# Causal mask of a 16-head attention as 26 more contraction rows of the score products, in place of mask matmuls

## The reference

```
att = jnp.einsum('bthd,bThd->bhtT', q, k) / math.sqrt(HD)
causal = jnp.triu(jnp.ones((Tx, Tx), bool), 1)
att = jnp.where(causal, -jnp.inf, att)
att = jax.nn.softmax(att, axis=-1)
out = jnp.einsum('bhtT,bThd->bthd', att, v).reshape(Bx, Tx, Cx)
return out @ Wo + bo
```

## Time and profile before

| | |
|---|---|
| median of 3 runs | 1179.05 us (1177.37 to 1180.38) |
| profiled execution: first to last instruction | 1175.3 us |
| profiled execution: its own time | not listed apart; the three runs lie 2.1 to 5.1 us above the span |
| PE / DVE / ACT / POOL busy, share of the span | 91% / 63% / 51% / 40% |
| attention of layer 0 | about the first 474 us of the span |
| mean granted PE clock | 0.953 of full |

### The profile page before, as it was taken

One profiled execution on the slowest core, in us unless ns is written; L12 is line 12 of the kernel. 1 busy time (PEld: TensorE's weight loads), 2 busy tenths in 40 slices (PEclk: granted clock), 3 DMA queues, 4 the chain that ended last, 5 costly groups with the idle time before them and its releaser, 6 DMA issues. The chain is left out here.

```text
span 1175.3 us, 19800 instructions
## 1 busy us (share of the span) xinstructions
PE 1067.3 (91%) x6630; PEld 603.4 (51%) x6630; DVE 734.6 (63%) x1549; ACT 596.7 (51%) x1133; POOL 467.8 (40%) x692
## 2 busy tenths in 40 slices
PE   5699999999999998479999974899999998999997
PEld 3244455454454443336565642566666665455654
DVE  2867878787787783624332322767787874566756
ACT  3167667676767666113332322443444442876752
POOL 2444635444453511068888874323333420000000
PEclk9599999999999999579999996999999998999999
DMA  4531414233250411436766672021210002001001
GB/s 150 99 58 18 87 37 89 65 70 82 52 105 21 73 40 47 155 103 138 162 162 135 138 154 71 6 65 42 76 39 26 35 15 95 1 10 63 28 28 54
DMA packets 73540, 85.05 MB, mean 72 GB/s; under 512 B 12560, under 2 KB 67800, under 8 KB 73312
## 3 DMA queue, kind: packets, MB, share of 16 engines
q1 hardware_dynamic: 61088, 66.99, 21.9%
q0 software_dynamic: 12288, 16.79, 8.4%
q10 hardware_dynamic: 64, 0.02, 0.0%
HBM read 45.31 MB, written 25.21 MB: 60 GB/s over the span
## 5 line engine op out<-in xcount | busy, mean ns | idle before, releaser
L566 DVE TENSOR_REDUCE nmax<-psum 128x1 f32<-128x512 f32 (+3 forms) x352 | 215.6, 637 | 44.6 <-PE psum L790 39.8
L683 ACT ACTIVATE pT<-psum 128x512 f32<-128x512 f32 x320 | 181.2, 596 | 65.5 <-PE psum L811 35.5
L788 PE MATMUL psum<-k6T,q6T 96*128 96x512 bf16 (+3 forms) x512 | 128.7, 312 | 15.2 <-DVE nmax L566 11.3
L808 PE MATMUL psum<-q6T,k6T 99*128 99x512 bf16 x320 | 119.3, 382 | 1.1 <-ACT pT L683 0.9
L1093 POOL DMA_INDIRECT residual<-expert_y,idx_e x64 | 101.3, 1583 | 25.2 <-issue 17.1
L1612 DVE TENSOR_TENSOR l_scores<-psum,const_sb 128x512 f32<-128x512 f32 x128 | 79.5, 684 | 19.1 <-PE psum L1787 19.0
L788 PEld LDWEIGHTS psum<-k6T,q6T 96*128 96x128 bf16 x512 | 46.0, 100 | 88.4 <-DVE nmax L566 55.2
L790 PE MATMUL psum<-negs_bf,ident_bf 128*128 128x128 bf16 (+2 forms) x352 | 89.0, 253 | 0.0
L823 PE MATMUL psum<-pT,v 128*32 128x512 f32 x640 | 85.0, 604 | 0.0
L1080 POOL DMA_INDIRECT expert_tokens<-router_input,idx_e x64 | 63.2, 987 | 50.0 <-POOLq L913 30.8
L1745 PE MATMUL psum<-l_hT,l_w 128*128 128x512 f32 x128 | 66.4, 643 | 1.6 <-ACT l_hT L1680 0.9
(11 more groups left out here) (298 smaller groups left out, 2245.4 us busy)
## 6 DMA issues: line engine op xcount, KB each, us to landing
q6T<-q_parts SPq DMA_DIRECT2D x96, 128.0 KB, 4.3
expert_w<-in_ew SPq DMA_DIRECT2D x16, 768.0 KB
x_in<-in_x SPq DMA_DIRECT2D x8, 512.0 KB, 4.2
residual<-x SPq DMA_DIRECT2D x32, 128.0 KB, 1.9
router_input<-h SPq DMA_DIRECT2D x32, 128.0 KB, 1.8
l_x<-residual SPq DMA_DIRECT2D x8, 512.0 KB, 6.6
x_dram<-l_x SPq DMA_DIRECT2D x32, 128.0 KB, 1.7
out<-c_out SPq DMA_DIRECT2D x16, 256.0 KB, 2.1
```

What stands on the lines that cost most here:

```text
L566: dve.tensor_reduce(nmax[:, i, u * nh:(u + 1) * nh], ps_s[:, n % SR, 0:nh * (i + 1) * P].rearrange("p (h k) -> p h k", h=nh), AX_X, ALU.ma ...
L683: act.activation(pT[:, n % PR].rearrange("p h t -> p (h t)"), ps_t[:, n % TR, :], ACT.Exp, scale=HD ** -0.5).then_inc(probs, 1)
L788: pe.matmul(out[:, a, :], q6T[0:6 * HD, b % 2, u * nh + a, i * P:(i + 1) * P], k6T[0:6 * HD, b % 2, 0:w], start=a == 0, stop=False, skip_g ...
L808: last = pe.matmul(out, k6T[:, b % 2, j * P:(j + 1) * P], q6T[:, b % 2, hg * 4:hg * 4 + 4, i * P:(i + 1) * P], start=True, stop=j < i)
```

## The change

The mask moves into the contraction. 26 more rows (96 to 121) are added to `q6T` and `k6T`; the three rows of maxima move to 122 to 124. On the query side these rows hold powers of two that depend only on a query's place in its tile; on the key side they hold powers of two of the other sign, so that the product is hugely negative where the key is after the query. The 128 places are cut into 5 segments of 26 or 25.

- S: the mask product L790 is gone. The product of each head has 122 contraction rows in place of 96.
- ST on the diagonal: L811 is gone. In its place the product is split in two, over segments 0, 2, 4 (3 x 26 queries of 4 heads) and segments 1, 3 (2 x 25 queries), each with key tiles of its own.
- `k6T` now has 15 tiles of 128 per sequence buffer: masked, plain, even-segment and odd-segment copies of the keys. ACT fills them with three copies per sequence (L747, L748, L751 of the new kernel) where there was one.
- At the start one more DMA brings the mask constants, POOL writes them with 11 casts in front of its first `st` step, and SP places the query rows in `q6T` with two DMAs in front of the list of steps.
- Two DVE casts and a DVE memset at the start go.

```diff
-        k6T = sb("k6T", [6 * HD + 3, 2, T], BF16)
+        k6T = sb("k6T", [P, 2, K_TILES * P], BF16)
+        mask = sb("mask_rows", [P, 5, P])
+        phi = sb("mask_queries", [P, T], BF16)
...
+def parted(v, first, count):
+
+    lo, size = SEGMENTS[first]
+    return bass.AP(v.tensor, v.offset + lo * v.ap[-1][0], [list(v.ap[0]), list(v.ap[1]), [51 * v.ap[-1][0], count], [v.ap[-1][0], size]])
...
+                sp.wait_ge(mask_ready, 1)
+                for s in range(2):
+                    sp.dma_start(q6T[K_ROWS:MASK_ROWS, s], phi[K_ROWS:MASK_ROWS, :].unsqueeze(1).to_broadcast(
+                        [MASK_ROWS - K_ROWS, H, T])).then_inc(mask_placed[s], 16)
...
+                pool.wait_ge(mask_loaded, 16)
+                settle(pool, m.passed)
+                pool.tensor_copy(phi[K_ROWS:P, :].rearrange("p (i t) -> p i t", i=NT),
+                                 mask[K_ROWS:P, 4:5, :].to_broadcast([P - K_ROWS, NT, P])).then_inc(mask_ready, 1)
+                for s in range(2):
+                    for n, at, count_of in ((0, own_tile(0), 3), (0, own_tile(3), 1), (1, plain_tile(0), 3), (2, even_tile(0), 4),
+                                            (3, odd_tile(0), 4)):
+                        pool.tensor_copy(k6T[K_ROWS:P, s, at * P:(at + count_of) * P].rearrange("p (i t) -> p i t", i=count_of),
+                                         mask[K_ROWS:P, n:n + 1, :].to_broadcast([P - K_ROWS, count_of, P])).then_inc(mask_ready, 1)
+                pool.wait_ge(mask_ready, 11)
+                settle(pool, m.passed)
                 pool.wait_ge(ready, 1)
...
-                        act.activation(k6T[0:6 * HD, b % 2, :], ps_x[0:6 * HD, x_use[s] % XR].bitcast(BF16)[:, 0:T],
+                        turned = ps_x[0:K_ROWS, x_use[s] % XR].bitcast(BF16)
+                        act.activation(k6T[0:K_ROWS, b % 2, 0:plain_tile(0) * P], turned[:, 0:plain_tile(0) * P], ACT.Copy)
+                        act.activation(k6T[0:K_ROWS, b % 2, plain_tile(0) * P:even_tile(0) * P], turned[:, 0:T],
                                        ACT.Copy).then_inc(x_drain, 1)
+                        act.wait_ge(x_drain, x_use[s] + 1)
+                        act.activation(k6T[0:K_ROWS, b % 2, even_tile(0) * P:K_TILES * P].rearrange("p (two t) -> p two t", two=2),
+                                       k6T[0:K_ROWS, b % 2, plain_tile(0) * P:even_tile(0) * P].unsqueeze(1).to_broadcast([K_ROWS, 2, T]),
+                                       ACT.Copy).then_inc(keys_masked, 1)
...
                         for a in range(nh):
-                            pe.matmul(out[:, a, :], q6T[0:6 * HD, b % 2, u * nh + a, i * P:(i + 1) * P],
-                                      k6T[0:6 * HD, b % 2, 0:w], start=a == 0, stop=False, skip_group_check=True)
-                        pe.matmul(out[:, :, i * P:w], m.ident_bf[:], m.negs_bf[:].unsqueeze(1).to_broadcast([P, nh, P]),
-                                  start=False, stop=True, skip_group_check=True).then_inc(s_fill, 1)
+                            last = pe.matmul(out[:, a], q6T[0:MASK_ROWS, b % 2, u * nh + a, i * P:(i + 1) * P],
+                                             keys[:, first:first + step_by * i + 1:step_by, :], start=a == 0, stop=True,
+                                             skip_group_check=True)
+                        last.then_inc(s_fill, 1)
...
-                        last = pe.matmul(out, k6T[:, b % 2, j * P:(j + 1) * P],
-                                         q6T[:, b % 2, hg * 4:hg * 4 + 4, i * P:(i + 1) * P], start=True, stop=j < i)
-                        if j == i:
-                            last = pe.matmul(out, m.ident_bf[:], m.negt_bf[:].unsqueeze(1).to_broadcast([P, 4, P]),
-                                             start=False, stop=True)
-                        last.then_inc(t_fill, 1)
+                        queries = q6T[0:ALL_ROWS, b % 2, hg * 4:hg * 4 + 4, i * P:(i + 1) * P]
+                        if j < i:
+                            pe.matmul(out, keys(plain_tile(j)), queries, start=True, stop=True).then_inc(t_fill, 1)
+                        else:
+                            pe.wait_ge(keys_masked, b + 1)
+                            pe.matmul(parted(out, 0, 3), keys(even_tile(i)), parted(queries, 0, 3), start=True, stop=True,
+                                      skip_group_check=True)
+                            pe.matmul(parted(out, 1, 2), keys(odd_tile(i)), parted(queries, 1, 2), start=False, stop=True,
+                                      skip_group_check=True).then_inc(t_fill, 1)
```

More of the change, by code:

```diff
@@ L31 @@
 EPS = 1e-5
-NEG = -1e30
 ROWS, ROW_GATE_A, ROW_SHIFT_B, ROW_SCALE_B, ROW_GATE_B, ROW_GATE_L1 = 5, 0, 1, 2, 3, 4
@@ L36 @@
 C_IDENT, C_ROPE = 0, 128
-C_NEGS = C_ROPE + NT * 2 * HD
-C_NEGT, C_KEEP, C_BD, C_SEQ, C_SGN, C_PARITY, C_HEADS = (C_NEGS + n for n in (128, 256, 384, 512, 513, 514, 516))
+C_KEEP = C_ROPE + NT * 2 * HD
+C_BD, C_SEQ, C_SGN, C_PARITY, C_HEADS = (C_KEEP + n for n in (128, 256, 257, 258, 260))
 C_SPREAD = C_HEADS + KC * 32
@@ L56, in rope_rows, with own_tile, plain_tile, even_tile @@
     return np.repeat(table, P // HD, axis=1).transpose(1, 0, 2)
+SEGMENTS = ((0, 26), (26, 25), (51, 26), (77, 25), (102, 26))
+K_ROWS = 6 * HD
+MASK_ROWS = K_ROWS + 26
+ALL_ROWS = MASK_ROWS + 3
+K_TILES = 15
+def own_tile(i):
+    return i if i < NT - 1 else 2 * NT - 2
+def plain_tile(j):
+    return NT - 1 + j
+def even_tile(i):
+    return 2 * NT - 1 + i
+def odd_tile(i):
+    return 3 * NT - 1 + i
+def mask_rows():
+    MID, STEP = 54, 27
+    n = MASK_ROWS - K_ROWS
+    c = np.zeros((5, 32, P), np.float64)
+    s = np.arange(P)
+    def masks(chosen, exponents, out):
+        for r in range(n):
+            at = [lo + r for lo, size in (SEGMENTS[j] for j in chosen) if r < size]
+            passed = sum((s > t).astype(int) for t in at)
+            for k, e in zip(range(1, len(at) + 1), exponents if len(at) == len(exponents) else exponents[::2]):
+                out[r, passed == k] = -2.0 ** (e - MID)
+    masks(range(5), [19 + STEP * j for j in range(5)], c[0])
+    masks((0, 2, 4), [26, 26 + 2 * STEP, 19 + 4 * STEP], c[2])
+    masks((1, 3), [26 + STEP, 26 + 3 * STEP], c[3])
+    for j, (lo, size) in enumerate(SEGMENTS):
+        for r in range(size):
+            c[4, r, lo + r] = 2.0 ** (MID - STEP * j)
+    c[0:4, n:n + 3] = 1
+    return c.transpose(1, 0, 2).astype(np.float32)
 def shape_constants():
@@ L195, in attention_phase @@
         c_loaded = sem("att_c_loaded")
+        mask_loaded = sem("att_mask_loaded")
+        mask_ready = sem("att_mask_ready")
+        keys_masked = sem("att_masked_keys_ready")
+        mask_placed = [sem(f"att_mask_placed{s}") for s in range(2)]
         mod_loaded = [sem(f"att_wmod_loaded{n}") for n in range(2)]
@@ L226, in attention_phase @@
         qs = sb("q_parts", [P, 2, 3, T], BF16)
-        q6T = sb("q6T", [6 * HD + 3, 2, H, T], BF16)
+        q6T = sb("q6T", [P, 2, H, T], BF16)
         nmax = sb("nmax", [P, NT, H])
@@ L351, in _ @@
                 sp.dma_start(wmod[:, :, 0:2 * C], m.d["wmod"][:, 0, :, 0:2 * C]).then_inc(mod_loaded[0], 16)
-                sp.dma_start(m.const[:, 0:C_NEGS], m.d["const"][:, 0:C_NEGS]).then_inc(const_loaded[0], 16)
+                sp.dma_start(m.const[:, 0:C_KEEP], m.d["const"][:, 0:C_KEEP]).then_inc(const_loaded[0], 16)
+                sp.dma_start(mask[K_ROWS:P], m.d["mask"]).then_inc(mask_loaded, 16)
                 for dst, name in early:
                     sp.dma_start(dst[:], m.d[name]).then_inc(w_loaded[0], 16)
-                sp.dma_start(m.const[:, C_NEGS:C_END], m.d["const"][:, C_NEGS:C_END]).then_inc(const_loaded[1], 16)
+                sp.dma_start(m.const[:, C_KEEP:C_END], m.d["const"][:, C_KEEP:C_END]).then_inc(const_loaded[1], 16)
                 sp.dma_start(wmod[:, :, 2 * C:6 * C], m.d["wmod"][:, 0, :, 2 * C:6 * C]).then_inc(mod_loaded[1], 16)
@@ L780, in step @@
                         if first_scores[b, u * nh // 8] == s:
+                            pe.wait_ge(mask_ready, 11)
+                            pe.wait_ge(mask_placed[b % 2], 16)
                             pe.wait_ge(x_drain, x_use[("kT", b)] + 1)
@@ L785, in step @@
                         w = (i + 1) * P
-                        out = ps_s[:, n % SR, 0:nh * w].rearrange("p (h k) -> p h k", h=nh)
+                        out = ps_s[:, n % SR, 0:nh * w].rearrange("p (h k t) -> p h k t", h=nh, t=P)
+                        keys = k6T[0:MASK_ROWS, b % 2, :].rearrange("p (k t) -> p k t", t=P)
+                        first, step_by = own_tile(i), 1
+                        if i == NT - 1:
+                            first = plain_tile(0)
+                        if i == 1:
+                            step_by = plain_tile(0) - own_tile(1)
                         for a in range(nh):
-                            pe.matmul(out[:, a, :], q6T[0:6 * HD, b % 2, u * nh + a, i * P:(i + 1) * P],
```

(10 more changed lines are left out.)

15 lines of the change are left out of this document (5 added, 10 removed).

## The result

The kernel after took 1157.82 us (median of 4 runs, 1157.64 to 1161.28), the kernel before 1179.38 in the same session (1177.37 to 1180.38). The ratio is 0.9832 with the interval 0.9816 to 0.9849: 19.8 us faster by the ratio and 21.6 by the medians, where 25.3 was forecast. The profiled execution is the slowest of the four (1161.28 us, span 1159.4), at a mean granted clock of 0.949 where the other three had 0.954 to 0.956.

The account below looks back on a forecast made before the run. The prediction took PE to bound the steady attention, with DVE 10.5 us behind. Gains of 35.1 us less additions of 5.4, 2.4 and 2.0 gave -25.3 from 1179.05, so 1154 us, range 1138 to 1168.

Parts of the forecast that it names:

- PE is the bound before, and removing 7.0 us of it helps: Steady attention: PE busy 51.53 of 52.60 us a period; the mask products removed are 7.0 us per sequence.
- I take 48.0, near the DVE end: Period of the steady attention: 48.0 us, between 45.6 and 48.3; gain 4.6 per period, 27.6 over six.
- At 45.6 DVE would be 92% busy without any of its waits: Reason given for a period near the DVE end, 48.0 us, instead of the 45.6 with PE still the bound.
- The part behind the last key copy, 4.1 + 0.9: Last sequence after its key copy: 4.1 us gained on remaining score steps, 0.9 on eight diagonal steps.
- I take 2.5, between 0 and 7.0: First sequence's scores, before the key copy of sequence 1: 2.5 us gained, between 0 and 7.0.
- Casts on POOL, +5.4: Start: eleven casts ahead of POOL's first step add 5.4 us uncovered, between 3.3 and 9.8.
- ACT copies, +2.4: Three key copies instead of one delay queued exponentials: 0.3 us per sequence, between 0 and 1.7; in all +2.4.
- The split pair, +2: Diagonal ST steps: uneven run starts cost 0.015 us per step over 128 steps, +2; upper end +82.
- PE stays the bound: Rival for the steady attention: DVE's S waits end with PE's masks; 1131 to 1135 us, chance 0.12.
- The ring rival: DVE and ACT steps keep their places, holding PE at 50 us a period, copies at full cost; 1165 to 1179, chance 0.14.
- The slow pair: Rival: split diagonal products run slowly, deciding from 0.21 us excess a step; 1234 us at the f32 end, chance 0.06.
- the change without effect: Rival: PE waits at every S for its bank, freed time becomes waits, only additions stay; 1189 us, chance 0.02.

Follow-up runs that it names:

- masks_gone: The kernel before without both mask products (causal mask left out) and with nothing added: 1150.8 us, ratio 0.9771.
- q_late_before: The kernel before with DVE's query products moved behind up to two reductions, nothing else: 1171.9 us, ratio 0.9937.
- combo: The changed kernel with mask casts behind POOL's first st step, query products behind up to two reductions, third key copy in ACT's gap: 1134.3 us.
- dve_short3: The changed kernel with DVE's S reduction reading only the first half of each head's keys: 1152.7 us, ratio 0.9794.
- q_late3: The changed kernel with each DVE query product moved behind up to two following S reductions or h2 steps: 1144.9 us, ratio 0.9716.
- pool_late3: The changed kernel with POOL's eleven mask casts behind its first st step instead of in front: 1152.9 us, ratio 0.9786.
- third_gap3: The changed kernel with ACT's third key copy moved into its wait between the two query casts: 1153.3 us, ratio 0.9790.
- no_third: The changed kernel without the third key copy, the diagonal pair reading the plain keys (mask left out of ST): 1151.6 us, ratio 0.9793.
- one_pair: The changed kernel with the split diagonal pair as one 512-column product on the plain keys (mask left out of ST): 1155.0 us, ratio 0.9800.
- combo4: combo with DVE's query products allowed behind up to four reductions or h2 steps instead of two: 1135.7 us, ratio 0.9645.

## Why the prediction was right, and where its sizes were off

**PE is the bound before, and removing 7.0 us of it helps.** Right in the main. PE was busy 98% of a period, and masks_gone shows 4.1 us less a period from the removal alone. But 1.1 of the 52.1 us was already DVE's order (q_late_before), so PE alone would have allowed 44.0 or less, and the prediction's 45.6 for that case was too high. That combo stands at 45.7 is partly coincidence.

**"I take 48.0, near the DVE end."** The term was mis-sized: 48.8 measured. The additions hold 0.75 of it (48.80 against 48.05 in masks_gone), so the removal by itself came to 48.05 where 48.0 was forecast. Moving the third copy gives 0.54 back, so most of the 0.75 is that copy, which I had priced at 0.3 per sequence in a term of its own. And I counted 4.6 from the late period of 52.6, six times, though the mean of the six was 52.1; the first one took only 50.6. The gain was 20.0 instead of 27.6: 4.8 of the difference is the new period, 2.8 the old one.

**"At 45.6 DVE would be 92% busy without any of its waits."** The value chosen was near, but this reason failed, so that the number is near is luck. The period is not held by DVE's load: dve_short3 took it to 67% and gained 0.5 us a period. What holds it are two stalls in DVE's fixed order, one behind the other: the wait at the query product, while a reduction stands ready behind it, and then the h instruction, which takes 1.5 us in place of 0.5 beside a POOL instruction. PE waits 0.66 us for the reduction behind the first and 0.79 behind the second. I had written that the wait would shrink little, which is what happened (20.3 to 19.5 us), but took it as a fixed cost beside the load and not as a cause of the 48; the second stall isn't in the prediction at all. With both removed, in combo, DVE runs at 38.82 of 45.80 us, 85%, and PE hardly waits. q_late3 and combo removed them together, and no run removed one alone.

**The part behind the last key copy, 4.1 + 0.9.** 5.0 measured, from that copy to the router. The two terms were not measured apart.

**"I take 2.5, between 0 and 7.0", the part in front of sequence 1's copy.** In the profiled execution it lies outside the stated bounds: 1.3 us lost. The row to read was the clock. The windows from the first score to the copy of sequence 1, of before and of masks_gone (the clock is the third number from the right):

```profile
34.00:79.80 45.80, 37.08 (x183) 17.16 (x183) 32.33 (x59) 16.91 (x31) 22.80 (x43) 0.74 0.38 74
```

```profile
33.70:82.50 48.80, 36.25 (x131) 13.66 (x132) 31.84 (x59) 17.04 (x31) 22.79 (x43) 0.62 0.40 73
```

With work only removed, this stretch became 3 us longer, at a mean clock of 0.62 instead of 0.74; in after it was 0.67 and 47.1 us. Windows of 1 and 5 us show why. Before, the granted clock was at full (2.4 GHz) for good from 61 us on, 27 us behind the first score. In after it reached full at 66 us, also 26 us behind the first score, but fell back to half (1.2 GHz) at 72 and was at full for good only from 80 us on:

```profile
70.00:75.00 5.00, 4.12 (x13) 1.70 (x14) 4.40 (x8) 2.52 (x5) 3.72 (x7) 0.73 0.01 2
75.00:80.00 5.00, 5.00 (x17) 2.69 (x16) 0.57 (x1) 2.77 (x6) 1.58 (x2) 0.59 0.51 90
```

The kernels that give PE as little work fall into two groups. In pool_late3, third_gap3, no_third and dve_short3 the clock is at full for good 26 to 28 us behind the first score, and the stretch takes 44.1 to 44.8 us. In masks_gone, after, one_pair, q_late3, combo and combo4 it falls back once more and is at full for good 37 to 41 us behind it, and the stretch takes 45.8 to 48.8 us. So less work on PE doesn't lose the time by itself; the late fall of the clock goes with 1 to 5 us. What decides it is not shown: from 65 to 70 us PE was busy 3.45 of 5 us in after, where the clock then fell, and 3.36 in third_gap3, where it did not. It may differ between executions of one kernel: the three others of after had 0.006 more mean clock over about 1159 us, an estimate of 14 us less at half clock (0.006 x 1159 / 0.5), and were 3.3 to 3.6 us shorter than the profiled one. They have no trace, and the 2.5 may have been right for them.

**Casts on POOL, +5.4.** 5.7 by the first score, 5.0 by the run that moves them. The rate from the 16 and 64 element casts gave 5.4 for a stretch that took 5.15. The two-input end, 9.8, was far off. The mask DMA was in time, as forecast: the first cast starts at 7.98, no later than POOL's first step before (8.04).

**ACT copies, +2.4.** The third copy alone, by third_gap3 and no_third, is 4.5 to 5.0 us by the times (no_third 4.6 by the ratio), and 5.9 and 6.8 at the end in the profiles, part of which is the first stretch above. The copies were shorter than I took (1.06 for the 1024 elements instead of 1.26); the price is the two ST banks behind them, as at 89.41.

**The split pair, +2.** 0.24 us against 0.22; by one_pair's period under 1 us in all. On runs of 25 and 26 columns the trace doesn't agree with the rule of the Trainium skill's page "Advanced Engine Details and Errata", section "Memory Cachelines", that non-contiguous patterns slow matmuls significantly; it is compatible with the half of it that asks for two consecutive elements.

**Rivals.** PE stays the bound (1131 to 1135) is what the change could have been: combo lands in that range at 1134.3, with three moves around it. The ring rival (1165 and up) named the right mechanism, steps that keep their places, with too large a price: it put the period at 50. The slow pair and the change without effect are excluded by the pair's 0.24 us and the 352 missing instructions. The additions together were priced at 9.8 us, and measured 7 by the times and 9.6 by the profiles.

**The sum.** By the events the attention gained 18.0 where the sum said 25.3. The difference of 7.3 is 7.6 in the periods, 3.8 in the stretch ahead of them and 0.3 at the start, less the 4.4 for copies and pairs, which the measured events already contain. By the medians the gain was 21.6, since the profiled execution is 3.5 us above the other three: the forecast of 1154 was 3.8 us too low. That it came so near owes something to luck: the 4.4 for copies and pairs, counted beside a period that already held them, took back more than half of the 7.6 that the periods were overrated by. Of its signs, POOL's first step (13.61 for 13.5), the first score (39.76 for 39.5) and the copies (0.48, 0.59, 1.06) came as written, DVE's share came out at 84% for 88%, and the pair's first product took 0.15 for 0.13.

## What to carry to other kernels

When work leaves the engine that bounds a kernel, look next for the blocking waits in the fixed order of the engine behind it, not for its busy share: here one waiting instruction moved behind two ready ones was worth 13 us, and a fifth of that engine's work 5. Look also for instructions of one line with two durations: part of those 13 us may be a DVE instruction that no longer ran beside POOL. Set-up work that a change brings belongs behind the first step of the start's chain, and extra copies into a gap in which their engine waits anyway; here the two moves gave back 5.0 and 4.5 us. Count a saved stretch from the mean of its repetitions, not from the one that was looked at.

## What was not expected of the hardware

The same DVE instruction took two durations. Groups of DVE from 130 to 360 us, of after and then of combo (mean ns of one behind the total):

```profile
L682 DVE SCALAR_TENSOR_TENSOR h<-h,rstd,rowb 128x256 f32<-128x256 f32 x19 | 18.2, 960 | 0.7
```

```profile
L685 DVE SCALAR_TENSOR_TENSOR h<-h,rstd,rowb 128x256 f32<-128x256 f32 x20 | 9.7, 485 | 0.7
```

Before it was 957 as well. The timeline of POOL in after, over the one at 215.83 that took 1.51 us:

```profile
215.79 1.27 POOL L494 TENSOR_TENSOR q_turned<-q_product,q_swapped 128x512 f32<-128x512 f32 x1 [0.27 <-POOL q_swapped L491]
```

POOL's instruction ends at 217.06 and DVE's at 217.34, 0.28 us later. The mean of 960 hides two values: two of the four L682 of a period take 0.48, and the two behind the query products 1.47 and 1.51. All twelve long ones from 150 to 300 us, six in this trace and six in before, began while such a POOL instruction ran and ended 0.28 or 0.29 us behind it. The DVE instruction ahead of it (L679, at 215.24) shows the same in small: it took 0.56 instead of 0.48 and ended at 215.80, 0.28 behind this one:

```profile
214.25 1.27 POOL L491 TENSOR_TENSOR q_swapped<-q_swapped,rope_sb 128x512 f32<-128x512 f32 x1 [2.25 <-ACT q_swapped L727]
```

The query product, which reads PSUM, took 0.75 beside POOL and 0.74 in q_late3. With the product moved, DVE is through with L682 before POOL starts these. It fits what the Trainium skill says on the page "SBUF — State Buffer", section "Terms": the shared port pair is held for a whole instruction, and the loser blocks. It is worth about 2 us a period of DVE's time (4 x 0.48), part of what q_late3 gained. No run separated it from the wait, so its share stays open.

The granted clock in the stretch from the first score to the copy of sequence 1 had a mean between 0.62 and 0.73 over kernels that give PE nearly the same work there, and the stretch took 44.1 to 48.8 us, the ones above 45 us with a late fall of the clock back to half. In the steady part the clock stayed at 1.00 although PE idled 6%.
